# Two graph attention layers on one core: six row maxima of layer 1 moved into layer 0's fourth chunk, and one epilogue moved from GpSimd to VectorE

## The chip, the cores and the metric

The kernel runs on one core of one Trainium2 chip. The metric is the device time of one execution in microseconds (us); lower is better. Time before: 656.13 us, the median of 3 runs (655.10 to 657.52).

## What is computed

Two attention layers over one dense adjacency of 4096 x 4096 int32, each with a residual and a layer norm over 64 features.

```python
def _L0_gnn_ref(item_embs, entity_embs, adj, W, a):
    Wh = item_embs @ W
    We = entity_embs @ W
    scores = (Wh @ a1)[:, None] + (We @ a2)[None, :]
    e = jnp.where(scores > 0, scores, ALPHA * scores)
    e = jnp.where(adj > 0, e, NEG_BIG)
    attention = jax.nn.softmax(e, axis=1)
    return jax.nn.elu(attention @ entity_embs + item_embs)
...
def _L1_gnn_ref(x, edge_index, weight_w, weight_a, bias):
    wh = x @ weight_w
    e = (wh @ a_src)[:, None] + (wh @ a_dst)[None, :]
    e = jax.nn.leaky_relu(e, negative_slope=0.01)
    attention = jax.nn.softmax(jnp.where(edge_index > 0, e, NEG_INF), axis=1)
    return attention @ wh + bias
...
x = _layernorm(x + _L0_gnn_ref(x, L0_gnn_entity_embs, adj, L0_gnn_W, L0_gnn_a), axis=-1)
x = _layernorm(x + _L1_gnn_ref(x, adj, L1_gnn_weight_w, L1_gnn_weight_a, L1_gnn_bias), axis=-1)
```

## The kernel before

**Chunks and steps.** The 4096 rows of a layer are 32 tiles of 128 rows. A layer is done in five chunks of 4, 8, 8, 8 and 4 tiles (`WIDTHS`). Chunks are numbered through both layers: 0 to 4 are layer 0, 5 to 9 layer 1 (`NC` is 5). A chunk has 32 steps J, one for each tile of 128 columns of the adjacency. The position in the code of all that stands beside a step is written out by hand as "if J is so much".

**A step.** TensorE writes the mask of the step into PSUM (`zps`, line 1161): the adjacency in fp8 (`v`) times diagonals `D` of one value a row, 4 or 8 matmuls. Then the row score `S_row` and the column score go in, by one of two ways. In an unseeded step VectorE does it after the mask (`z`, line 990). In a seeded step ScalarE has written it before (a seed, line 718), and TensorE adds the mask to it. `SEEDS` has the number of seeded steps of each chunk. ScalarE takes the exponential into `Pm` (line 726), and TensorE multiplies it with the features (the product, lines 1106 and 1113) two steps later, in narrow chunks up to four or five. `zps` is a ring of three places of two banks; a narrow step takes one bank.

**Row maxima.** The diagonals of a chunk need for each row the maximum of `u` (the column scores) over its neighbours. `row_max(C, r, q)` (line 847, VectorE) takes it for row tile r of chunk C over one segment q of the 4096 columns, with `v` and `u_row` as inputs; `segments` has their bounds. Layer 0's `u_row` is known from the start. In layer 1 a piece of `u` is known only when its rows of layer 0 are finished, so chunks 5 and 6 have four and three segments. `pieces_at(C, J)` says which pieces stand at which step. The maxima of the next chunk are done during a chunk; before the change, those of layer 1 stand in chunk 4 and later, since both layers use the same `u_row`: the first loads of layer 1's `u` wait until layer 0's last maximum is done. `diagonals(C + 1)` follows at J=30, and TensorE begins the next chunk with them.

**The adjacency.** SP loads halves of row tiles (1 MB) into three buffers `adj_in`; VectorE (a compare, line 824) or ScalarE turns each into fp8 in `v`. In chunk 3 VectorE compares the eight halves of chunk 4's rows (`halves_at`, spread over 27 steps).

**The epilogue of a chunk** runs during the next one. ScalarE copies the sums out (`o`, J=4); GpSimd then adds the flags' part, multiplies with the reciprocal, and with relu and exponential by ScalarE makes the elu, subtracts the mean, squares, takes the power -0.5 of the variance (line 543) and scales (line 510). VectorE gives it the reciprocal (`reciprocal`), the sums (`sums`) and the squares (`squares`) at the steps in the tables `AFTER_WIDE`, `IN_LAST` (chunk 4) and `IN_FIRST` (chunk 5). With `scores` VectorE makes the next layer's scores of these rows (`uS`). At step `rows` TensorE turns `uS` (`turn_rows`, line 1025). Chunks 3 and 4 (`SPREAD`) have no time for a round through memory: VectorE makes diagonals of `u` (`u_diagonals`, line 904), TensorE spreads them (`spread_u`, line 1040), and ScalarE saves them in `u_row` (line 607). For chunks 0 to 2 the row goes to memory (`store_rows`) and is loaded to all partitions (`load_u`, line 420).

**What waits for what.** Each engine works through its own list in order. TensorE's `turn_rows` waits for `uS`, and every later mask and product stands behind it.

## Time and profile before

| | us |
|---|---|
| median of the runs | 656.13 |
| profiled execution | 654.75 |
| its span | 652.9 |
| VectorE, ScalarE, TensorE, GpSimd busy | 565.0, 522.3, 507.9, 180.6 |

The profile is of one execution. Busy shares are means over stages that differ, so a step is read in its own stretch. Times of rows are from the span's start. Chunk 3 begins (first exponential) at 258.5 us, chunk 4 at 325.1, chunk 5 at 382.8, chunk 6 at 435.9.

### The profile page before, as it was taken

How to read it: one execution, taken by the hardware profiler on the slowest of the kernel's cores; microseconds unless marked ns; L12 is line 12 of the kernel's file. 1: busy time of each engine (PE TensorE's matmuls, PEld its weight loads, DVE VectorE, ACT ScalarE, POOL GpSimd, SP SyncE). 2: the span in 40 equal slices, each digit the busy share in tenths (PEclk: the TensorE clock that was granted, in tenths of full speed). 3: DMA queues.
4: the chain of work that ended last, by engine and by line, in shares of the span. 5: the costliest groups of instructions: out<-in, count | busy, mean ns of one | idle time of the engine just before them, and what ended most of it. 6: DMA issues, size and time to landing. Idle time of an engine off the chain costs nothing. (4 is left out here: it accounts for less than half of the span.)

```text
span 652.9 us, 14284 instructions
## 1 busy us (share of the span) xinstructions
PE 507.9 (78%) x6039; PEld 236.0 (36%) x6039; DVE 565.0 (87%) x761; ACT 522.3 (80%) x606; POOL 180.6 (28%) x126
## 2 busy tenths in 40 slices
...
DMA packets 18252, 76.16 MB, mean 117 GB/s; under 512 B 6300, under 2 KB 8524, under 8 KB 9996
## 3 DMA queue, kind: packets, MB, share of 16 engines
...
q10 hardware_dynamic: 532, 0.08, 0.1%
q14 instruction: 17, 0.14, 0.1%
...
## 5 line engine op out<-in xcount | busy, mean ns | idle before, releaser
L726 ACT ACTIVATE Pm<-zps,ebias 128x1024 f32<-128x1024 f32 (+1 forms) x320 | 291.8, 934 | 75.0 <-DVE zps L990 47.4
L847 DVE CUSTOM_DVE_ANT_0 junk<-v,u_row 128x2048 int8<-128x2048 int8 (+4 forms) x144 | 308.1, 2159 | 3.3 <-ACT v L586 3.0
L1161 PE MATMUL zps<-D,v 128*128 128x128 bf16 x2048 | 166.5, 225 | 57.9 <-DVE D L867 27.7
L1161 PEld LDWEIGHTS zps<-D,v 128*128 128x128 fp8e4 x2048 | 119.5, 100 | 199.6 <-ACT zps L718 76.0
L718 ACT ACTIVATE zps<-S_row,ntau_col 128x1024 f32<-128x1024 f32 (+1 forms) x191 | 180.9, 949 | 5.1
L990 DVE SCALAR_TENSOR_TENSOR zps<-S_row,tau_col,zps 128x1024 f32<-128x1024 f32 (+1 forms) x129 | 135.0, 1064 | 42.8 <-PE zps L1161 42.0
L1106 PE MATMUL acc<-Pm,VE 128*32 128x512 f32 (+2 forms) x1280 | 150.5, 544 | 15.7 <-ACT Pm L726 13.1
L1106 PE MATMUL acc<-Pm,X 128*32 128x512 f32 (+2 forms) x1280 | 139.4, 524 | 20.8 <-ACT Pm L726 19.2
L1113 PE MATMUL acc<-Pm,ones 128*32 128x256 f32 (+1 forms) x1280 | 88.6, 350 | 0.0
L477 POOL TENSOR_TENSOR tAB<-flag,totW 128x520 f32<-128x520 f32 (+1 forms) x9 | 12.1, 1349 | 253.4 <-issue 161.6
L1113 PEld LDWEIGHTS acc<-Pm,ones 128*32 128x32 f32 x1280 | 43.5, 116 | 73.9 <-issue 64.9
L824 DVE TENSOR_SCALAR v<-adj_in 128x2048 fp8e4<-128x2048 int32 x44 | 61.7, 1405 | 1.9 <-DMA adj_in<-in_adj 1.8
L586 ACT ACTIVATE v<-adj_in,tanh_bias 128x2048 fp8e4<-128x2048 int32 x20 | 39.7, 2004 | 12.1 <-DMA adj_in<-in_adj 12.1
L1106 PEld LDWEIGHTS acc<-Pm,X 128*32 128x32 f32 x1280 | 28.3, 109 | 45.9 <-ACT Pm L726 31.7
L1106 PEld LDWEIGHTS acc<-Pm,VE 128*32 128x32 f32 x1280 | 27.5, 112 | 35.8 <-ACT Pm L726 22.2
L543 POOL TENSOR_TENSOR rstd<-var,mhalf 128x8 f32<-128x8 f32 (+1 forms) x10 | 21.9, 2192 | 45.1 <-DVE var L915 45.1
L506 POOL TENSOR_TENSOR tAB<-tAB,mean 128x512 f32<-128x512 f32 (+1 forms) x9 | 18.6, 2066 | 32.2 <-DVE mean L910 32.2
L489 POOL TENSOR_TENSOR o<-o,rden 128x512 f32<-128x512 f32 (+1 forms) x9 | 13.3, 1479 | 21.4 <-DVE rden L518 21.4
L485 POOL TENSOR_TENSOR o<-o,tAB 128x520 f32<-128x520 f32 (+1 forms) x9 | 12.4, 1378 | 21.3 <-ACT o L672 12.0
L507 POOL TENSOR_TENSOR tAB<-tAB 128x512 f32<-128x512 f32 (+1 forms) x9 | 16.2, 1804 | 0.7
L586 ACT ACT_TABLE_LOAD x1 | 1.3, 1283 | 18.4 <-DMA adj_in<-in_adj 18.4
L1025 PE MATMUL zps<-identf,uS 128*8 128x128 f32 (+1 forms) x5 | 1.6, 314 | 17.9 <-DVE uS L933 17.9
...
## 6 DMA issues: line engine op xcount, KB each, us to landing
...
S_row<-S_rows_scratch SPq DMA_DIRECT2D x3, 256.0 KB, 3.0
out<-tAB SPq DMA_DIRECT2D x3, 256.0 KB, 3.3
...
u_row<-u_row_scratch SPq DMA_DIRECT2D x2, 256.0 KB, 3.5
S_row<-S_rows_scratch POOLq DMA_DIRECT2D x1, 256.0 KB, 8.4
...
```

What stands on the lines that cost most here:

```text
L506: link(ns.tensor_tensor(tBf, tBf, per_row(mean[:, 0:n]), ALU.add))
L507: ns.tensor_tensor(tAf, tBf, tBf, ALU.mult).then_inc(sq_done, 1)
L543: g.tensor_tensor(rstd[:, 0:R(C)], var[:, 0:R(C)], mhalf[:, 0:R(C)], ALU.pow).then_inc(rstd_done, 1)
L586: a.activation(v[:, H // 2, H % 2 * HALF:(H % 2 + 1) * HALF], adj_in[:, H % AB, :], ACT.Tanh, bias=tanh_bias[:, :], scale=40.0, saturate=F ...
L718: a.activation(mask_of(n), S_row[:, C % 2, 0:R(C) * P], ACT.Relu, bias=ntau_col[:, layer(C), n % JT:n % JT + 1]).then_inc(seed_done, 1)
L726: a.activation(Pm_of(k, 0, R(C) * P), mask_of(k), ACT.Exp, bias=ebias[:, layer(C), int(seeded(k)), J:J + 1])\
L824: d.tensor_scalar(v[:, H // 2, H % 2 * HALF:(H % 2 + 1) * HALF], adj_in[:, H % AB, :], 0.0, 0.5, ALU.is_gt, ALU.subtract, saturate=False). ...
L847: d.tensor_tensor_reduce(out=junk[:, at % 2, 0:cols.stop - cols.start], in0=v_bytes[:, rt, cols], in1=u_row[:, cols], scale=1.0, scalar=-3 ...
L990: d.scalar_tensor_tensor(z, S_row[:, C % 2, 0:R(C) * P], tau_col[:, layer(C), J:J + 1], z, ALU.max, ALU.add).then_inc(z_done, 1)
L1106: last = t.matmul(acc[s * F + f:s * F + f + G, int(second), 0:cols], V[:, f:f + G], Pm_of(k, s * w, cols), start=first, stop=end)
L1113: last = t.matmul(acc[q * G:(q + 1) * G, 1, 0:w], ones[:, :], Pm_of(k, q * w, w), start=first, stop=end)
L1161: last = t.matmul(mask[:, r * P:(r + 1) * P], v[:, chunks[C][1] + r, J * P:(J + 1) * P], D[:, C % 2, PART * second + r, :], start=(r * P % ...
```

## The change

Layer 1's `u_row` gets a place of its own: the buffer of `adj_in` that half 61 was in, free once that half is converted. So six of the maxima of chunks 5 and 6, over the columns of chunks 0 and 1 (1536), stand in chunk 3 at `BEFORE_LAST`. Segments are cut at row 1536 instead of 1280 and 2048. Chunk 4's halves and maxima are spread over 20 steps of chunk 3 instead of 27 and 29. The epilogue of chunk 3 is done by VectorE: `epilogue` is split in `add_up`, `normalise` and `scale`, which stand at J=6, 10 and 15 of chunk 4; GpSimd keeps the power. `rows` goes from 23 to 20 in chunk 4 and from 17 to 20 in chunk 5. Chunk 3 has 20 seeded steps (16 before), chunk 5 has 20 (26 before). Unseeded are then in chunk 3 the steps 0 to 3, 5, 7, 11, 15, 19, 23, 27 and 28, in chunk 4 the steps 0, 1, 7, 8 and 22 to 25, in chunk 5 the steps 0 to 3, 6 to 8, 17 and 22 to 25.

```diff
-SEEDS = ((29, 28, 28, 16, 24), (26, 18, 18, 10, 0))
+SEEDS = ((29, 28, 28, 20, 24), (20, 18, 18, 10, 0))
...
-    IN_LAST = dict(reciprocal=6, elu=9, sums=13, squares=17, scores=21, rows=23)
-
-    IN_FIRST = dict(reciprocal=6, elu=8, sums=10, squares=13, scores=15, rows=17, maxima=19, second=21)
+    IN_LAST = dict(add_up=6, elu=8, normalise=10, scores=15, rows=20)
+
+    IN_FIRST = dict(reciprocal=6, elu=8, sums=10, squares=14, scores=18, rows=20, maxima=21, second=23)
...
-    EARLY = (4, 5, 7, 8, 9, 10, 11, 12, 14, 15, 18, 19, 22, 24)
+    BEFORE_LAST = (19, 20, 21, 23, 25, 27)
+    EARLY = (3, 4, 5, 7, 8, 11, 12, 13, 17, 19)
+    LATE_AT = 23
...
+    BY_VECTOR = (NC - 2, LAST)
...
-        u_row = sb("u_row", [P, N], BF16)
+        U1_AT = (2 * JT - 3) % AB
+        u_row = sb("u_row", [P, N], BF16), adj_in[:, U1_AT, :].bitcast(BF16)
...
-        um = sb("um", [P, 2, RT, Q])
+        um = sb("um", [P, 3, RT, Q])
...
+            third, first_spread = rows(2).start, rows(SPREAD[0]).start
             if C == NC:
-                first_spread = rows(SPREAD[0]).start
-                ends = [0, first_spread // 2, first_spread, KNOWN * P, N]
+                ends = [0, third, first_spread, KNOWN * P, N]
             elif C == NC + 1:
-                ends = [0, QW, KNOWN * P, N]
+                ends = [0, third, KNOWN * P, N]
...
-            return [h for h in range(first, end) if (h - first) * 27 // (end - first) == J]
+            return [h for h in range(first, end) if (h - first) * halves_within(C) // (end - first) == J]
+
+        def halves_within(C):
+
+            return 20 if C == NC - 2 else 27
+
+        known_first = [(NC, r, 0) for r in range(R(NC))] + [(NC + 1, r, 0) for r in range(R(NC + 1))]
...
+            if C == NC - 2:
+                n = 2 * R(nxt)
+                return [(nxt, i // 2, i % 2) for i in range(n) if i * halves_within(C) // n + 1 == J] + \
+                       [piece for piece, step in zip(known_first, BEFORE_LAST) if step == J]
             if C == NC - 1:
-                early = [(NC, r, q) for q in range(2) for r in range(R(NC))] + [(NC + 1, r, 0) for r in range(R(NC + 1))]
-                late = [(NC, r, 2) for r in range(R(NC))]
+                early = [(NC, r, 1) for r in range(R(NC))] + known_first[len(BEFORE_LAST):]
                 return [piece for piece, step in zip(early, EARLY) if step == J] + \
-                       [piece for i, piece in enumerate(late) if at("rows", C) + 2 + i == J]
+                       [(NC, r, 2) for r in range(R(NC)) if LATE_AT + r == J]
             if C == NC:
                 n = R(nxt)
-                open_ = [(nxt, r, 0) for r in range(len(EARLY) - 2 * R(NC), n)] + [(nxt, r, 1) for r in range(n)]
-                return [piece for i, piece in enumerate(open_) if 1 + i * 18 // len(open_) == J] + \
+                return [(nxt, r, 1) for r in range(n) if 1 + r * 18 // n == J] + \
                        [(NC, r, 3) for r in range(R(NC)) if at("maxima", C) + r // 2 == J] + \
...
             def load_u(C):
-                sp.dma_start(u_row[:, rows(C)], u_scr[rows(C)].rearrange("(one n) -> one n", one=1)
+                wait_v(sp, 2 * JT - 3)
+                sp.wait_ge(scr_written, written(max(C + 1, 2)))
+                sp.dma_start(u_row[1][:, rows(C)], u_scr[rows(C)].rearrange("(one n) -> one n", one=1)
                              .broadcast_to([P, R(C) * P])).then_inc(u_landed[C], 16)
...
+                if C == NC - 2:
+                    for c in range(2):
+                        load_u(c)
                 if 1 <= C < NC - 1:
                     store_rows(C - 1)
                     load_S(C + 1)
                 elif C == NC - 1:
-                    sp.wait_ge(max_done, 2 * JT)
-                    sp.wait_ge(scr_written, written(SPREAD[0]))
-                    for c in range(SPREAD[0]):
-                        load_u(c)
+                    load_u(2)
                     load_S(C + 1)
                     store_rows(C - 1)
...
+        def add_up(eng, ns, link, C):
...
-            if C == LAST:
+            if C in BY_VECTOR:
                 reciprocal(C)
...
+            ns.tensor_tensor(tBf, h, xs, ALU.add).then_inc((elu_in, y_done)[layer(C)], 1)
+
+        def normalise(eng, ns, link, C, sums, squares):
...
-            (squares if C == LAST else inverse)(C)
+            if C in BY_VECTOR:
+                squares(C)
+
+        def scale(eng, ns, C):
...
+            ns.tensor_tensor((xs, tBf)[layer(C)], tBf, per_row(rstd, C), ALU.mult).then_inc(new_done, 1)
...
-                if C == LAST:
+                if C in BY_VECTOR:
                     inverse(C)
-                else:
-                    epilogue(pool, g, link, C, inverse=inverse)
+                    continue
+                add_up(pool, g, link, C)
+                normalise(pool, g, link, C, None, None)
+                inverse(C)
+                scale(pool, g, C)
...
-                act.wait_ge(max_done, 2 * JT)
-                a.activation(u_row[:, rows(C)], zps[:, buf("u", C), 0:R(C) * P], ACT.Copy).then_inc(u_saved, 1)
+                wait_v(act, 2 * JT - 3)
+                a.activation(u_row[1][:, rows(C)], zps[:, buf("u", C), 0:R(C) * P], ACT.Copy).then_inc(u_saved, 1)
...
-                                       in0=v_bytes[:, rt, cols], in1=u_row[:, cols], scale=1.0, scalar=-3.0e38,
-                                       op0=ALU.mult, op1=ALU.max, accum_out=um[:, C % 2, r, q:q + 1])\
+                                       in0=v_bytes[:, rt, cols], in1=u_row[layer(C)][:, cols], scale=1.0, scalar=-3.0e38,
+                                       op0=ALU.mult, op1=ALU.max, accum_out=um[:, C % 3, r, q:q + 1])\
...
                 if C in SPREAD:
-                    xs = X[:, xc, 0:F]
-                    per_feature = [wbc[:, k, :].unsqueeze(1).broadcast_to([P, R(C), F]) for k in (2, 3)]
+                    if C in BY_VECTOR:
+                        scale(dve, d, C)
...
-                        if J == at("reciprocal", C) + BEHIND_FIRST * (C - 1 in FIRSTS):
+                        if J == at("add_up", C):
+                            add_up(dve, d, link, C - 1)
+                        if J == at("normalise", C):
+                            normalise(dve, d, link, C - 1, sums, squares)
+                        if at("reciprocal", C) and J == at("reciprocal", C) + BEHIND_FIRST * (C - 1 in FIRSTS):
```

VectorE, chunk 3, from the `z` of step 18 (before) or 19 (now) to the scores of chunk 2. `ISA junk,um` is a row maximum, `ISA um` its read-out, `v<-adj_in` a compare. Before:

```order
L990 SCALAR_TENSOR_TENSOR zps<-S_row,tau_col,zps 128x1024
L847 ISA junk,um<-v,u_row 128x2048
L847 ISA um 128x1
L824 TENSOR_SCALAR v<-adj_in 128x2048
L990 SCALAR_TENSOR_TENSOR zps<-S_row,tau_col,zps 128x1024
L928 TENSOR_REDUCE s_col<-tAB 128x8
L930 TENSOR_REDUCE t_col<-tAB 128x8
L932 TENSOR_SCALAR uS<-t_col,uoff 128x8
L933 TENSOR_SCALAR uS<-s_col 128x8
L847 ISA junk,um<-v,u_row 128x2048
L847 ISA um 128x1
L990 SCALAR_TENSOR_TENSOR zps<-S_row,tau_col,zps 128x1024
```

Now:

```order
L1027 SCALAR_TENSOR_TENSOR zps<-S_row,tau_col,zps 128x1024
L879 ISA junk,um<-v,adj_in 128x1536
L879 ISA um 128x1
L879 ISA junk,um<-v,adj_in 128x1536
L879 ISA um 128x1
L879 ISA junk,um<-v,adj_in 128x1536
L879 ISA um 128x1
L961 TENSOR_REDUCE s_col<-tAB 128x8
L963 TENSOR_REDUCE t_col<-tAB 128x8
L965 TENSOR_SCALAR uS<-t_col,uoff 128x8
L966 TENSOR_SCALAR uS<-s_col 128x8
L1027 SCALAR_TENSOR_TENSOR zps<-S_row,tau_col,zps 128x1024
```

Three maxima over 1536 columns, whose row lies in `adj_in`, stand ahead of the scores; the compare and the maximum over 2048 columns that stood there went to earlier steps.

VectorE, chunk 4, from J=6. `rden` is the reciprocal, `tAB` and `o` are the epilogue's tiles. Before:

```order
L518 RECIPROCAL rden<-o 128x8
L990 SCALAR_TENSOR_TENSOR zps<-S_row,tau_col,zps 128x512
L847 ISA junk,um<-v,u_row 128x1280
L847 ISA um 128x1
L990 SCALAR_TENSOR_TENSOR zps<-S_row,tau_col,zps 128x512
L847 ISA junk,um<-v,u_row 128x1280
L847 ISA um 128x1
L847 ISA junk,um<-v,u_row 128x1280
L847 ISA um 128x1
L847 ISA junk,um<-v,u_row 128x1280
L847 ISA um 128x1
L847 ISA junk,um<-v,u_row 128x1280
```

Now:

```order
L498 TENSOR_TENSOR tAB<-flag,totW 128x520
L506 TENSOR_TENSOR o<-o,tAB 128x520
L542 RECIPROCAL rden<-o 128x8
L510 TENSOR_TENSOR o<-o,rden 128x8x64
L515 TENSOR_TENSOR tAB<-o,X 128x512
L1027 SCALAR_TENSOR_TENSOR zps<-S_row,tau_col,zps 128x512
L879 ISA junk,um<-v,adj_in 128x1024
L879 ISA um 128x1
L1027 SCALAR_TENSOR_TENSOR zps<-S_row,tau_col,zps 128x512
L879 ISA junk,um<-v,adj_in 128x1536
L879 ISA um 128x1
L522 TENSOR_TENSOR tAB<-tAB 128x512
```

Four passes of the epilogue stand around the reciprocal, and the first of `normalise` after two more maxima.

VectorE, chunk 4, ahead of the row scores that TensorE turns (`s_col`, `t_col`, `uS`). Before:

```order
L914 TENSOR_REDUCE tot<-tAB 128x8
L915 TENSOR_SCALAR var<-tot 128x8
L847 ISA junk,um<-v,u_row 128x2048
L847 ISA um 128x1
L847 ISA junk,um<-v,u_row 128x2048
L847 ISA um 128x1
L925 TENSOR_TENSOR tAB<-X,wbc 128x8x64
L926 TENSOR_TENSOR tAB<-X,wbc 128x512
L928 TENSOR_REDUCE s_col<-tAB 128x8
L930 TENSOR_REDUCE t_col<-tAB 128x8
L932 TENSOR_SCALAR uS<-t_col,uoff 128x8
L933 TENSOR_SCALAR uS<-s_col 128x8
```

Now:

```order
L879 ISA junk,um<-v,adj_in 128x1536
L879 ISA um 128x1
L879 ISA junk,um<-v,adj_in 128x1536
L879 ISA um 128x1
L538 TENSOR_TENSOR X<-tAB,rstd 128x8x64
L958 TENSOR_TENSOR tAB<-X,wbc 128x8x64
L959 TENSOR_TENSOR tAB<-X,wbc 128x512
L961 TENSOR_REDUCE s_col<-tAB 128x8
L963 TENSOR_REDUCE t_col<-tAB 128x8
L965 TENSOR_SCALAR uS<-t_col,uoff 128x8
L966 TENSOR_SCALAR uS<-s_col 128x8
L936 TENSOR_TENSOR D<-identb,uS 128x1024
```

`X<-tAB,rstd` (the scaling) came from GpSimd's list, and the squares stand three maxima ahead instead of two. On TensorE the turning of `uS` and the spreading of `u` stand before the masks of steps 20 and 21, not between those of steps 22 and 23.

## Rows read from the trace of the kernel before

**Rows 1.** The page, part 1: busy time, share of the span and instructions of each engine.
```profile
PE 507.9 (78%) x6039; PEld 236.0 (36%) x6039; DVE 565.0 (87%) x761; ACT 522.3 (80%) x606; POOL 180.6 (28%) x126
```

**Rows 2.** Busy time by stretch: length, each engine's busy us, TensorE's granted clock, DMA, GB/s.
```profile
258.50:325.07 66.57, 64.54 (x774) 28.62 (x775) 53.82 (x60) 54.90 (x58) 20.12 (x13) 1.00 0.30 98
325.07:382.80 57.73, 38.29 (x635) 23.05 (x631) 48.25 (x73) 38.73 (x64) 23.95 (x12) 0.87 0.04 11
382.80:435.90 53.10, 34.88 (x447) 17.05 (x440) 43.09 (x102) 36.94 (x64) 14.60 (x11) 0.88 0.04 11
...
356.50:367.90 11.40, 1.87 (x11) 0.84 (x15) 10.19 (x18) 0.70 (x2) 5.29 (x2) 0.56 0.00 0
```

**Rows 3.** The timeline of TensorE, chunks 3, 4 and 5: start, duration, line, idle before.
```profile
309.98 1.07 PE L1106 MATMUL acc<-Pm,VE 128*32 128x512 f32 x8
...
365.07 0.38 PE L1025 MATMUL zps<-identf,uS 128*8 128x128 f32 x1 [10.97 <-DVE uS L933]
...
412.49 0.37 PE L1025 MATMUL zps<-identf,uS 128*4 128x128 f32 x1 [6.89 <-DVE uS L933]
```

**Rows 4.** The timeline of ScalarE, chunk 4.
```profile
333.17 0.19 ACT L672 ACTIVATE o<-zps 128x8 f32<-128x8 f32 x1
...
340.41 0.63 ACT L680 ACTIVATE o<-tAB 128x512 f32<-128x512 f32 x1
340.95 0.67 ACT L718 ACTIVATE zps<-S_row,ntau_col 128x512 f32<-128x512 f32 x1
341.56 0.67 ACT L726 ACTIVATE Pm<-zps,ebias 128x512 f32<-128x512 f32 x1
...
368.65 1.00 ACT L607 ACTIVATE u_row<-zps 128x1024 bf16<-128x1024 f32 x1
```

**Rows 5.** The timeline of GpSimd, chunks 3 and 4.
```profile
301.27 1.19 POOL L514 TENSOR_TENSOR tAB<-X,wbc 128x512 f32<-128x512 f32 x1
...
356.67 3.76 POOL L543 TENSOR_TENSOR rstd<-var,mhalf 128x8 f32<-128x8 f32 x1 [1.00 <-DVE var L915]
360.51 1.53 POOL L510 TENSOR_TENSOR X<-tAB,rstd 128x512 f32<-128x512 f32 x1
```

**Rows 6.** The timeline of VectorE, chunk 4: scores of chunk 3 and what follows.
```profile
362.07 0.69 DVE L925 TENSOR_TENSOR tAB<-X,wbc 128x512 f32<-128x512 f32 x1 [0.93 <-POOL X L510]
...
364.71 0.23 DVE L932 TENSOR_SCALAR uS<-t_col,uoff 128x8 f32<-128x8 f32 x1
...
367.06 2.28 DVE L847 CUSTOM_DVE_ANT_0 junk<-v,u_row 128x2048 int8<-128x2048 int8 x1
...
380.58 0.73 DVE L867 TENSOR_SCALAR D<-identb,g 128x128 bf16<-128x128 bf16 x4
```

**Rows 7.** The same timeline: one instruction of each kind that is counted.
```profile
291.44 1.28 DVE L990 SCALAR_TENSOR_TENSOR zps<-S_row,tau_col,zps 128x1024 f32<-128x1024 f32 x1
...
372.25 1.22 DVE L847 CUSTOM_DVE_ANT_0 junk<-v,u_row 128x1024 int8<-128x1024 int8 x1
...
373.40 0.75 DVE L990 SCALAR_TENSOR_TENSOR zps<-S_row,tau_col,zps 128x512 f32<-128x512 f32 x1
...
389.40 2.28 DVE L847 CUSTOM_DVE_ANT_0 junk<-v,u_row 128x2048 int8<-128x2048 int8 x1
...
394.80 1.76 DVE L847 CUSTOM_DVE_ANT_0 junk<-v,u_row 128x1536 int8<-128x1536 int8 x1
```

**Rows 8.** VectorE's waits from 258.5 to 301 (us, times, longest); a slowed maximum; the scores.
```profile
DVE zps L990 <- PE zps L1161: 4.2, 5, 1.4
...
282.13 3.20 DVE L847 CUSTOM_DVE_ANT_0 junk<-v,u_row 128x2048 int8<-128x2048 int8 x1
...
301.93 0.68 DVE L928 TENSOR_REDUCE s_col<-tAB 128x8 f32<-128x512 f32 x1
```

**Rows 9.** The page, part 6: issues, KB each, median us to landing.
```profile
u_row<-u_row_scratch SPq DMA_DIRECT2D x2, 256.0 KB, 3.5
```

**Rows 10.** The timeline of VectorE, end of chunk 5.
```profile
432.30 1.39 DVE L867 TENSOR_SCALAR D<-identb,g 128x128 bf16<-128x128 bf16 x8
```

More of the change, by code:

```diff
@@ L457, in _, with tiles_of, per_row, per_feature @@
             sp.wait_ge(out_written, stored(LAST))
-        def epilogue(eng, ns, link, C, sums=None, squares=None, inverse=None):
+        def tiles_of(C):
             n = R(C)
-            b3 = [P, n, F]
-            xs = X[:, xcols(C), 0:F]
-            h, tAf, tBf = o[:, 0:n, 0:F], tA[:, 0:n, 0:F], tB[:, 0:n, :]
-            def per_row(t):
-                return t.unsqueeze(2).broadcast_to(b3)
-            def per_feature(t):
-                return t.unsqueeze(1).broadcast_to(b3)
+            return X[:, xcols(C), 0:F], o[:, 0:n, 0:F], tA[:, 0:n, 0:F], tB[:, 0:n, :]
+        def per_row(t, C):
+            return t[:, 0:R(C)].unsqueeze(2).broadcast_to([P, R(C), F])
+        def per_feature(t, C):
+            return t.unsqueeze(1).broadcast_to([P, R(C), F])
+        def add_up(eng, ns, link, C):
+            n = R(C)
+            xs, h, tAf, tBf = tiles_of(C)
             eng.wait_ge(totW_saved, layer(C) + 1)
@@ L500, in epilogue @@
                 ns.tensor_tensor(tBf, tBf, h, ALU.add).then_inc(y_done, 1)
-            else:
-                ns.tensor_tensor(tBf, h, xs, ALU.add).then_inc(y_done, 1)
-            if C == LAST:
+            if C in BY_VECTOR:
                 sums(C)
             eng.wait_ge(mean_done, C + 1)
-            link(ns.tensor_tensor(tBf, tBf, per_row(mean[:, 0:n]), ALU.add))
+            link(ns.tensor_tensor(tBf, tBf, per_row(mean, C), ALU.add))
             ns.tensor_tensor(tAf, tBf, tBf, ALU.mult).then_inc(sq_done, 1)
-            (squares if C == LAST else inverse)(C)
+            if C in BY_VECTOR:
+                squares(C)
+        def scale(eng, ns, C):
+            xs, h, tAf, tBf = tiles_of(C)
             eng.wait_ge(rstd_done, C + 1)
-            ns.tensor_tensor(xs if layer(C) == 0 else tBf, tBf, per_row(rstd[:, 0:n]), ALU.mult).then_inc(new_done, 1)
-            if layer(C) == 0 and C not in SPREAD:
-                eng.wait_ge(new_done, C + 1)
-                ns.tensor_tensor(tAf, xs, per_feature(wbc[:, 2, :]), ALU.mult).then_inc(sprod_done, 1)
-                ns.tensor_tensor(tBf, xs, per_feature(wbc[:, 3, :]), ALU.mult).then_inc(tprod_done, 1)
+            ns.tensor_tensor((xs, tBf)[layer(C)], tBf, per_row(rstd, C), ALU.mult).then_inc(new_done, 1)
         def reciprocal(C):
@@ L565, in _ @@
                     g.memset(columns_of_ones, 1.0).then_inc(ones_set, 1)
-                if C == LAST:
+                if C in BY_VECTOR:
                     inverse(C)
-                else:
-                    epilogue(pool, g, link, C, inverse=inverse)
+                    continue
[3 more added lines that the diff above has]
+                scale(pool, g, C)
+                if layer(C) == 0 and C not in SPREAD:
+                    xs, h, tAf, tBf = tiles_of(C)
+                    pool.wait_ge(new_done, C + 1)
+                    g.tensor_tensor(tAf, xs, per_feature(wbc[:, 2, :], C), ALU.mult).then_inc(sprod_done, 1)
+                    g.tensor_tensor(tBf, xs, per_feature(wbc[:, 3, :], C), ALU.mult).then_inc(tprod_done, 1)
         @block.scalar
```

19 lines of the change are left out of this document (12 added, 7 removed).

## The prediction

> **What bounds the kernel now.** I read the page's busy shares first [rows 1]: VectorE is busy for 87% of the span, ScalarE 80%, TensorE 78%, and no one of them is the bound everywhere. So I cut the span where ScalarE's first exponential of a chunk begins and asked for busy times by stretch [rows 2]. Chunk 3 (258.5 to 325.1 us) belongs to TensorE: 64.5 of 66.6 us busy at full clock, with VectorE at 53.8 and ScalarE at 54.9. Chunk 4 (325.1 to 382.8) belongs to nobody: TensorE 38.3 of 57.7, VectorE 48.3, ScalarE 38.7. In its stretch from 356.5 to 367.9, TensorE works 1.9 us and ScalarE 0.7. Chunk 5 (53.1 us) is alike.
>
> TensorE's waits name what is missing [rows 3]: it stands before line 1025, the turning of the row scores, for `uS` of VectorE, 10.97 us in chunk 4 (at J=23, from 354.10 to 365.07) and 6.89 us in chunk 5 (at J=17, until 412.49). `uS` is the end of chunk 3's epilogue: sums by ScalarE at 333.36 (333.17 + 0.19) [rows 4], then GpSimd until 362.04 (360.51 + 1.53) [rows 5], then the scores on VectorE, 362.07 to 364.94 [rows 6]. So GpSimd and its partners take 28.7 us for ten operations: its last pass of 128x512 took 1.53 us and the power of eight elements a row 3.76, while VectorE runs a pass of 128x512 in 0.69 [rows 5, 6].
>
> **The change in chunk 4, the term that decides.** I step along VectorE, the engine that now carries both jobs, with durations from [rows 6, 7], less some 0.08 by which one overlaps the next (372.25 + 1.22 is 373.47, the next starts at 373.40): a maximum over 1024 columns 1.14 us, over 1536 1.68, over 2048 2.20; `z` of 512 columns 0.66, of 1024 columns 1.19; a pass of 128x512 0.61, or 0.70 where it is linked, so that the next waits for its end (an estimate from the 0.69).
> - Until J=6 it does three maxima of 1024 in place of two of 1280, and is free by 330.1. The first product with the flags (0.7) fits before ScalarE's 333.36. Then add 0.7, reciprocal 0.25, multiply 0.7, add 0.6: 335.6.
> - J=7 to 9: two `z` and maxima of 1024 and 1536: 4.15 us, 339.8. ScalarE's relu is not done before 340.4 [rows 4], and its exponential by 341.0.
> - `normalise` at J=10: three passes (2.0), sums (0.9), two passes (1.3), squares (0.9) from 340.4: 345.6.
> - GpSimd's power: 3.76 us in [rows 5], beside VectorE's work, so to 349.4. Three maxima of 1536 (5.1) cover it: 350.7. That cover is thin by 1.3 us; without it VectorE would wait.
> - `scale` 0.7, two products 1.2, scores and `uS` as in [rows 6] 1.6: ready at 354.2, not 364.9. TensorE, now stopped at J=20, gets there some 3 us earlier than to J=23 (a seeded step takes ScalarE 1.3 us, [rows 4]), so it stands 3 to 4 us, not 11.
> - From there VectorE has the diagonals of `u` and the columns (2.2, from 364.9 to 367.1 in [rows 6]), two maxima of 1536 (3.4), four `z` (2.6), four maxima of 1024 (4.6), and `diagonals(5)` with its terms (2.4): 369.4. I add 0.7 for small gaps. The copy of `u` that the last four wait for ended at 369.65, 4.7 us after `uS` [rows 4, 6], so by 358.9, before VectorE asks for it at 361. Diagonals ready at 370.1 against 381.2 [rows 6]: **-11.1 us**. ScalarE has 12 exponentials (0.67) and six seeds (0.63) left after 357.2, 12 us, and ends at 369 to 370: no later. What is late next is VectorE itself.
>
> In columns, chunk 4 loses 8x1280 + 6x2048 and gains 4x1024 + 6x1536; the 9216 columns that are saved (about 10 us) went to chunk 3.
>
> **Chunk 3.** VectorE gets six maxima of 1536 (+10.1) and four fewer `z` of 1024 columns (-4.8); ScalarE four more seeds (+4.2, on 54.9 of 66.6). In sum it fits under TensorE. Where it may not: chunk 4's halves and maxima are pressed into 20 steps. Up to `scores` at J=22 VectorE has two more maxima of 2048 (4.4), one more compare (1.1), three new maxima (5.1), and three fewer `z` (-3.6): +7.0 us. The waits for TensorE before it, 4.2 us in five [rows 8], swallow some: it comes to `scores` 2.8 us later than at 301.9 [rows 8], near 305. Then `z` of step 23 is done near 308, its exponential near 309, and TensorE needs it at 310 (the product of step 23 at 309.98) [rows 3]. It fits barely; I take **+1.0 us**. Bounds: below, 0, since TensorE is already at 97%; above, the contention with GpSimd. A maximum of 2048 took 3.20 us at 282.13, beside GpSimd's passes, against 2.28 at 389.40 [rows 7, 8]. Six more slowed by 0.92 are 5.5, so +5.
> The Trainium skill (GPSIMD Engine Reference, 8. Key points) says that GpSimd contends with VectorE instructions that have two SBUF inputs or run in a two-port mode. The moved maxima have two such inputs, so by that rule all six pay if GpSimd works beside each, and the sum would be -4.6, not -10. The trace agrees that there is a price, but three of the six stand after GpSimd's last pass, which ended at 302.5 [rows 5].
>
> Loading: two of the three rows of `u` now leave SP at chunk 3's end of loads, before `store_rows(2)` and `load_S(4)`. They land in 3.5 us [rows 9], issued once half 61 is compared (J=12, about 283) and half 63 is issued, and are wanted at J=19, about 298. The third follows `store_rows(2)` and is wanted at chunk 4's J=3. Nothing waits, and `store_rows(2)` comes after both.
>
> **Chunk 5.** Six fewer seeds: ScalarE -3.8, VectorE +4.0 (six `z` of 0.66). VectorE was idle 10.0 of 53.1 us [rows 2]. The maxima keep their 16384 columns. Scores stand at J=18, behind two maxima of 2048 and the `z` of step 17: counted as above from the chunk's first exponential, `uS` is ready at +31.7 instead of +29.6 (412.4, [rows 3]). TensorE's wait grows from 6.9 to 8 or 9 us. But two maxima of 1536 that stood behind the scores (3.4 us) are done before. So the four maxima of 512 end at +38.8 (as before), and `diagonals(6)` at +51.0 (before +50.9, [rows 10]). **0 us**; bounds -2 (TensorE's low clock at its start goes) and +3 (VectorE full). Chunks 6 to 9 keep their order and durations: 0.
>
> **Sum:** -11.1 + 1.0 + 0 = -10.1, taken as -10. The profiled execution, 654.75 us around its span of 652.9, would take 644.8. The median of the runs is 656.13, 1.4 higher; by the same difference I predict 646.1. A measurement of this kernel can tell about 0.5%, 3.3 us, from no change: so faster means under 652.8.
>
> **The rivals.**
> - *Forecast*, -7 to -14: 0.72.
> - *VectorE in chunk 4 is late itself.* The ten passes cost 1.0 instead of 0.7, or GpSimd's power is not covered: `uS` at 359. The gain is half, -5, with chunk 3's +1: -4, 652.1. For it: 48.3 of 57.7 us were busy before. Against it: 28.7 us of epilogue shrink to some 7 us of passes, three reductions and one power. 0.11.
> - *Given back in chunks 3 and 5.* Chunk 3 +5, chunk 5 +4 (each `z` that leaves ScalarE lands in VectorE's chain): -2, 654.1. For it: `uS` in chunk 5 is late already. 0.10.
> - *Slower, through chunk 3.* Before J=22 stand 11 maxima and 8 compares. If all met GpSimd and lost 0.92 (for a compare an estimate from the maximum's): 19x0.92 = 17.5 us, of which three times 0.92 are there now. Less 1.5 us slack, TensorE would stand some 13 us in the one chunk that it bounds, and work after it at 1.2 GHz: the granted clock is 0.56 in the stretch of the 11 us wait, against 1.00 in chunk 3 [rows 2]. Ten us at the lower level cost 5. +18 - 11 = +7, 663. It decides from about 11 us lost in chunk 3. Against it: GpSimd is busy for 20.1 us of that chunk, and of its sixteen maxima and compares it slowed only three. 0.05. The Trainium skill (TensorE: Matmul & The Clock Gate, Part 1) has it that the low clock is the default and activity lifts it; the granted clocks above agree.
> - *The change doesn't do what it says*: the row of `u` lands late and VectorE stands at J=19. It must be 15 us late to matter. 0.02.
>
> **Numbers.** Faster: 0.72, and 0.08 of the second case. Same: the third, the rest of the second, half of the last: 0.14. Slower: 0.06. The range takes 641.5 (-14.6: chunk 5 gives 2, the clock stays up in chunk 4) to 653.0 (-3.1, second case and its surroundings); it leaves out the third and fourth, and tails.
>
> **What would show it.** TensorE's wait for `uS` in chunk 4 of 3 to 4 us, not 11; chunk 4 near 47 us long; chunk 3 66.6 to 69; chunk 5 53; in chunk 5 a longer wait; VectorE's maxima in chunk 4 all uncontended; GpSimd with ten ops fewer. Wrong if chunk 3 lengthens by over 5, if `uS` in chunk 4 comes later than 357, or if chunk 5 lengthens.

## The result, and the profile after

The changed kernel takes 652.12 us, median of 13 runs (649.99 to 653.74), against 656.02 for the kernel before, 13 runs beside it (652.40 to 657.52): a ratio of 0.9942, 95% interval 0.9926 to 0.9958. It is faster, by 3.9 us or 0.6%. The forecast was a gain of 10 us, 646.1. The profiled execution took 650.33 us, its span 648.5 against 652.9.

Busy times by stretch of the changed kernel, cut at the first exponential of chunks 3, 4, 5, 6 and 7. The columns are those of [rows 2]: length, TensorE's matmuls and weight loads, VectorE, ScalarE, GpSimd, granted clock, DMA.

```profile
258.20:329.89 71.69, 66.35 (x778) 29.21 (x775) 61.63 (x68) 59.44 (x63) 24.55 (x13) 0.98 0.28 91
329.89:375.60 45.71, 36.63 (x636) 23.10 (x637) 40.42 (x75) 38.45 (x65) 3.26 (x2) 0.96 0.04 13
375.60:428.69 53.09, 34.24 (x423) 17.03 (x420) 45.22 (x100) 35.72 (x62) 13.86 (x11) 0.84 0.03 11
428.69:494.14 65.45, 58.27 (x548) 23.25 (x544) 56.91 (x66) 55.19 (x57) 14.04 (x10) 0.92 0.04 11
```

Chunk 6 of the kernel before, the same view:

```profile
435.90:498.60 62.70, 53.09 (x536) 21.27 (x538) 56.95 (x66) 55.27 (x56) 14.03 (x10) 1.00 0.03 12
```

| | before | after | forecast | measured |
|---|---|---|---|---|
| chunk 3 | 66.6 | 71.7 | +1.0 (0 to +5) | +5.1 |
| chunk 4 | 57.7 | 45.7 | -11.1 | -12.0 |
| chunk 5 | 53.1 | 53.1 | 0 | 0.0 |
| chunk 6 | 62.7 | 65.4 | 0 | +2.8 |

With -0.3 us before chunk 3 that is -4.4, the difference of the spans. Chunks 7 to 9 are as they were. So the gain is where it was forecast, and a little larger; more than half of it is given back in two places, ahead of it and behind it.

**Chunk 4, the gain.** TensorE's two waits for `uS` in the changed kernel's timeline, which answer to [rows 3]:

```profile
358.57 0.27 PE L1064 MATMUL zps<-identf,uS 128*8 128x128 f32 x1 [3.64 <-DVE uS L966]
...
406.47 0.37 PE L1064 MATMUL zps<-identf,uS 128*4 128x128 f32 x1 [6.59 <-DVE uS L966]
```

3.64 us instead of 10.97, where 3 to 4 were expected.

**Chunk 3, the first loss.** VectorE around the scores of chunk 2, the changed kernel's timeline. L879 is a row maximum, L1027 a `z`, L961 the first reduction of `scores`:

```profile
275.94 3.25 DVE L879 CUSTOM_DVE_ANT_0 junk<-v,u_row 128x2048 int8<-128x2048 int8 x1
...
281.83 2.96 DVE L879 CUSTOM_DVE_ANT_0 junk<-v,u_row 128x2048 int8<-128x2048 int8 x1
...
300.78 2.66 DVE L879 CUSTOM_DVE_ANT_0 junk<-v,adj_in 128x1536 int8<-128x1536 int8 x1
...
303.37 2.73 DVE L879 CUSTOM_DVE_ANT_0 junk<-v,adj_in 128x1536 int8<-128x1536 int8 x1
...
306.03 1.75 DVE L879 CUSTOM_DVE_ANT_0 junk<-v,adj_in 128x1536 int8<-128x1536 int8 x1
...
307.71 0.67 DVE L961 TENSOR_REDUCE s_col<-tAB 128x8 f32<-128x512 f32 x1
...
309.35 1.28 DVE L1027 SCALAR_TENSOR_TENSOR zps<-S_row,tau_col,zps 128x1024 f32<-128x1024 f32 x1
```

ScalarE and TensorE behind it (L758 is the exponential, L750 a seed, L1145 the product, L1200 the mask):

```profile
310.67 1.12 ACT L758 ACTIVATE Pm<-zps,ebias 128x1024 f32<-128x1024 f32 x1 [3.27 <-DVE zps L1027]
311.81 1.12 ACT L750 ACTIVATE zps<-S_row,ntau_col 128x1024 f32<-128x1024 f32 x1
```

```profile
302.07 1.06 PE L1145 MATMUL acc<-Pm,VE 128*32 128x512 f32 x8 [1.38 <-ACT Pm L758]
...
312.99 1.03 PE L1200 MATMUL zps<-D,v 128*128 128x128 bf16 x8 [2.96 <-ACT zps L750]
```

The same mask in the kernel before:

```profile
309.43 0.62 PE L1161 MATMUL zps<-D,v 128*128 128x128 bf16 x8 [1.06 <-ACT zps L718]
```

VectorE reaches the scores at 307.7, not 305. The `z` of step 23 stands behind them; ScalarE waits 3.27 us for it, and its next seed, that of step 25, stands in ScalarE's list behind the exponential of step 23. TensorE waits for that seed: 2.96 us in the chunk that it bounds. The two waits make 4.3 us, and for 3.4 us from 312.5 the granted clock was low (0.98 on average over the chunk), worth up to 1.7. The wait of 1.1 us that stood at this place before is in the new one. 4.3 + 1.7 - 1.1 is 4.9 of the 5.1 us, an estimate, since the low clock may have cost less.

**Chunk 6, the second loss.** The table has chunk 5 at 53.1 us in both kernels, but inside it the changed one is ahead: its last exponential starts 48.1 us after its first (before 51.3). What sets the chunk's length is VectorE: the diagonals of chunk 6 are ready 50.4 us after the first exponential (before 50.9), and TensorE's first mask of chunk 6 waits for them. ScalarE waits behind it, in the changed kernel:

```profile
428.69 1.11 ACT L758 ACTIVATE Pm<-zps,ebias 128x1024 f32<-128x1024 f32 x1 [4.32 <-DVE zps L1027]
```

```profile
426.08 1.03 PE L1200 MATMUL zps<-D,v 128*128 128x128 bf16 x8 [2.06 <-DVE D L899]
```

Four stretches of the changed kernel: just before TensorE's clock falls, until it rises, the beginning of chunk 6, and a second fall inside it:

```profile
414.90:418.40 3.50, 1.59 (x28) 0.82 (x24) 3.33 (x15) 1.25 (x3) 0.00 (x0) 0.99 0.00 0
418.40:432.00 13.60, 10.67 (x91) 4.54 (x84) 9.79 (x32) 6.69 (x12) 0.00 (x0) 0.50 0.11 40
428.69:445.60 16.91, 14.57 (x112) 6.78 (x104) 12.87 (x11) 10.50 (x15) 0.00 (x0) 0.70 0.00 1
438.80:445.60 6.80, 6.80 (x41) 2.94 (x38) 4.93 (x5) 5.04 (x8) 0.00 (x0) 0.50 0.01 2
```

And the places in the kernel before that answer to the first three:

```profile
422.60:426.00 3.40, 1.76 (x28) 0.90 (x25) 3.12 (x16) 1.17 (x3) 0.00 (x0) 1.00 0.00 0
426.00:439.70 13.70, 10.68 (x138) 5.22 (x139) 12.00 (x34) 11.42 (x18) 0.00 (x0) 1.00 0.12 39
435.90:452.80 16.90, 13.20 (x140) 6.17 (x138) 15.58 (x14) 13.15 (x17) 2.50 (x3) 1.00 0.00 1
```

### The profile page after: what moved, and what is told of

Read it like the earlier page. It is cut to its first block, busy times and chain, and to the rows that moved or that the text cites. A ratio compares the mean times of both kernels' runs of the same rounds, so it can differ in the third digit from the quotient of the medians.

```text
span 648.5 us, 14276 instructions
## 1 busy us (share of the span) xinstructions
PE 511.5 (79%) x6037; PEld 237.8 (37%) x6039; DVE 567.1 (87%) x769; ACT 525.5 (81%) x608; POOL 163.6 (25%) x116
## 4 chain that ended last, share of the span: by engine, by line
DVE 28%; issue 26%; PE 19%; ACT 14%; POOL 6%; DMA 5%; SPq 1%; POOLq 0%; ACTq 0%; DVEq 0%
DVE junk L879 13%; PE acc L1145 10%; ACT Pm L758 10%; DVE zps L1027 7%; PE zps L1200 6%; DMA adj_in<-in_adj 5%; PE acc L1152 2%; DVE v L856 2%; ACT v L618 2%; ACT zps L750 1%; POOL o L506 1%; DVE tot L941 1%; POOL rstd L567 1%; POOL tAB L522 1%; DVE tot L946 1%
## 5 line engine op out<-in xcount | busy, mean ns | idle before, releaser
L758 ACT ACTIVATE Pm<-zps,ebias 128x1024 f32<-128x1024 f32 (+1 forms) x320 | 291.7, 936 | 68.5 <-DVE zps L1027 55.3
L1200 PE MATMUL zps<-D,v 128*128 128x128 bf16 x2048 | 168.2, 226 | 58.9 <-DVE D L899 27.9
L1200 PEld LDWEIGHTS zps<-D,v 128*128 128x128 fp8e4 x2048 | 121.0, 100 | 200.6 <-ACT zps L750 81.0
L750 ACT ACTIVATE zps<-S_row,ntau_col 128x1024 f32<-128x1024 f32 (+1 forms) x193 | 183.9, 955 | 5.1
L1027 DVE SCALAR_TENSOR_TENSOR zps<-S_row,tau_col,zps 128x1024 f32<-128x1024 f32 (+1 forms) x127 | 131.2, 1053 | 42.3 <-PE zps L1200 41.7
L1145 PE MATMUL acc<-Pm,VE 128*32 128x512 f32 (+2 forms) x1280 | 149.3, 540 | 16.3 <-ACT Pm L758 12.8
L1145 PE MATMUL acc<-Pm,X 128*32 128x512 f32 (+2 forms) x1280 | 143.4, 538 | 19.5 <-ACT Pm L758 18.0
L879 DVE CUSTOM_DVE_ANT_0 junk<-v,adj_in 128x2048 int8<-128x2048 int8 (+3 forms) x80 | 153.7, 1947 | 2.1 <-ACT adj_in L639 1.7
L879 DVE CUSTOM_DVE_ANT_0 junk<-v,u_row 128x2048 int8<-128x2048 int8 x64 | 152.6, 2398 | 2.5 <-ACT v L618 2.3
L1152 PEld LDWEIGHTS acc<-Pm,ones 128*32 128x32 f32 x1280 | 43.2, 115 | 73.2 <-issue 63.6
L1145 PEld LDWEIGHTS acc<-Pm,X 128*32 128x32 f32 x1280 | 28.9, 111 | 45.7 <-ACT Pm L758 30.4
L1145 PEld LDWEIGHTS acc<-Pm,VE 128*32 128x32 f32 x1280 | 27.3, 110 | 36.7 <-ACT Pm L758 24.1
L510 POOL TENSOR_TENSOR o<-o,rden 128x512 f32<-128x512 f32 (+1 forms) x8 | 10.8, 1346 | 24.4 <-DVE rden L542 24.4
L515 POOL TENSOR_TENSOR tAB<-o,X 128x512 f32<-128x512 f32 (+1 forms) x8 | 13.4, 1676 | 0.6
```

Of the source, the lines that this page charges most:

```text
L750: a.activation(mask_of(n), S_row[:, C % 2, 0:R(C) * P], ACT.Relu, bias=ntau_col[:, layer(C), n % JT:n % JT + 1]).then_inc(seed_done, 1)
L758: a.activation(Pm_of(k, 0, R(C) * P), mask_of(k), ACT.Exp, bias=ebias[:, layer(C), int(seeded(k)), J:J + 1])\
L879: d.tensor_tensor_reduce(out=junk[:, at % 2, 0:cols.stop - cols.start], in0=v_bytes[:, rt, cols], in1=u_row[layer(C)][:, cols], scale=1.0, ...
L1027: d.scalar_tensor_tensor(z, S_row[:, C % 2, 0:R(C) * P], tau_col[:, layer(C), J:J + 1], z, ALU.max, ALU.add).then_inc(z_done, 1)
L1145: last = t.matmul(acc[s * F + f:s * F + f + G, int(second), 0:cols], V[:, f:f + G], Pm_of(k, s * w, cols), start=first, stop=end)
L1152: last = t.matmul(acc[q * G:(q + 1) * G, 1, 0:w], ones[:, :], Pm_of(k, q * w, w), start=first, stop=end)
```

## The experiments

Theory 1 for chunk 3: the place of three maxima, ahead of the scores and beside GpSimd, costs the 5 us. Its rival: VectorE is full, wherever they stand. For chunk 4: which of the two edits, the maxima or the epilogue, made the gain. For chunk 6: the clock, or something that it accompanies. All ratios are to the kernel before, run beside.

### The maxima behind the scores

```diff
-    BEFORE_LAST = (19, 20, 21, 23, 25, 27)
+    BEFORE_LAST = (23, 24, 25, 26, 27, 28)
```

> The changed kernel, with the six moved maxima at J=23 to 28 of chunk 3, behind the scores of chunk 2, not at 19 to 27 with three of them ahead. Theory 1 (what costs chunk 3 its 5.1 us is that three maxima, two of them slowed by GpSimd from 1.68 to 2.6 and 2.7 us, stand ahead of the z of step 23, on which ScalarE's next seed and TensorE wait): VectorE reaches the scores some 5 us earlier, chunk 3 takes 66.6 to 68 us and not 71.7, none of the six maxima takes over 1.8 us, and the kernel is 3 to 5 us faster than the changed one (about 648). Theory 2 (VectorE is simply full in chunk 3 with six more maxima, wherever they stand): chunk 3 stays at 70 to 72 us and the time at 652.

647.08 us, ratio 0.9889 (0.9867 to 0.9912): some 0.5% better than the changed kernel, and the intervals do not overlap. (The profiled execution came to chunk 3 2.3 us later than that of the changed kernel, with the same code ahead of it. So lengths of chunks are compared, not spans.) Chunks 3 and 4:

```profile
260.50:328.10 67.60, 65.09 (x778) 28.74 (x775) 60.07 (x68) 59.36 (x63) 23.03 (x13) 1.00 0.30 97
328.10:374.10 46.00, 36.85 (x634) 23.16 (x635) 40.41 (x75) 38.39 (x64) 3.26 (x2) 0.93 0.04 13
```

All six moved maxima took 1.75 us. Chunk 3 is 1.0 us over the kernel before, with 6.3 us more of VectorE's work in it. Theory 1 holds; VectorE had the room. The halves and maxima of chunk 4 are still pressed into 20 steps here, so that is not what cost the 5 us.

### Chunk 2's two products on VectorE

The two GpSimd passes that ran beside the slowed maxima are taken away, and the maxima left where the change has them.

```diff
-                if layer(C) == 0 and C not in SPREAD:
+                if layer(C) == 0 and C < NC - 3:
...
-                if C in SPREAD:
+                if C in (NC - 3, NC - 2, NC - 1):
```

> The changed kernel (three moved maxima ahead of the scores), but the two products with the score weights in chunk 2's epilogue are VectorE's, as for chunks 3 and 4, not GpSimd's. These two passes ran beside the two slowed maxima. Theory 1 (GpSimd's passes slow the maxima): the maxima at J=19 and 20 take 1.75 us instead of 2.66 and 2.73; VectorE gains 1.9 and pays 1.2 for the products; chunk 3 is 70 to 71.5 us. Theory 2 (the maxima are slowed by something else, such as the adjacency's loads or the row's new place in adj_in): they stay at 2.6 to 2.7 us, and chunk 3 takes 72 to 73 us.

650.02 us, ratio 0.9919 (0.9892 to 0.9946). The maxima of J=19 and 20:

```profile
300.68 1.75 DVE L879 CUSTOM_DVE_ANT_0 junk<-v,adj_in 128x1536 int8<-128x1536 int8 x1
...
302.35 1.75 DVE L879 CUSTOM_DVE_ANT_0 junk<-v,adj_in 128x1536 int8<-128x1536 int8 x1
```

Theory 1 holds. The two were slowed by GpSimd, by 0.91 and 0.98 us, and by nothing else: the row in `adj_in` costs nothing. The Trainium skill (GPSIMD Engine Reference, 8. Key points) names this contention for instructions with two SBUF inputs; the trace agrees. Chunk 3 takes 70.8 us, 0.9 less, with 1.2 us of products added on VectorE. From that I estimate that the contention of these two is worth some 2 us. With the maxima behind the scores the chunk was 4.1 us shorter, so their place ahead of the scores is worth the other 2.

### Chunk 3 with its 16 seeds, maxima behind the scores

```diff
-SEEDS = ((29, 28, 28, 20, 24), (20, 18, 18, 10, 0))
+SEEDS = ((29, 28, 28, 16, 24), (20, 18, 18, 10, 0))
...
-    BEFORE_LAST = (19, 20, 21, 23, 25, 27)
+    BEFORE_LAST = (23, 24, 25, 26, 27, 28)
```

> As a_behind_scores, with 16 seeded steps in chunk 3 as before, not 20. VectorE gets four z of 1024 columns back (4.8 us), ScalarE loses four seeds. Theory 1 (behind the scores VectorE has room): chunk 3 67 to 69 us, the time within 1.5 us of a. Theory 2 (the four seeds are what made room for the six maxima): chunk 3 over 70 us and the time 3 to 5 us above a.

648.60 us, ratio 0.9909 (0.9888 to 0.9930). Chunk 3 takes 68.5 us, 0.9 more than with 20 seeds. In the profile the four seeds are worth about 1 us; the ratios, 0.9909 and 0.9889, overlap. The seeds are not what made room.

### The epilogue back on GpSimd, the maxima moved

```diff
-    IN_LAST = dict(add_up=6, elu=8, normalise=10, scores=15, rows=20)
+    IN_LAST = dict(reciprocal=6, elu=9, sums=13, squares=17, scores=21, rows=23)
...
-    LATE_AT = 23
+    LATE_AT = 25
...
-    BY_VECTOR = (NC - 2, LAST)
+    BY_VECTOR = (LAST,)
```

> The changed kernel, with the epilogue of chunk 3 back on GpSimd, its steps as before (reciprocal 6, elu 9, sums 13, squares 17, scores 21, rows 23) and the third segment's maxima at J=25 to 28. The moved maxima stay moved. Theory 1 (chunk 4's 12 us come from the epilogue on VectorE, which shortens TensorE's wait): TensorE waits 8 to 11 us for uS again, chunk 4 takes 54 to 57 us, time 661 to 663, slower than both kernels, since chunk 3's 5 us are paid for nothing. Theory 2 (they come from the 9216 columns of maxima that left chunk 4): chunk 4 takes 47 to 50 us and the time is near 654.

659.64 us, ratio 1.0070 (1.0041 to 1.0099): slower than both.

### The epilogue on VectorE, no maximum moved to chunk 3

```diff
-SEEDS = ((29, 28, 28, 20, 24), (20, 18, 18, 10, 0))
+SEEDS = ((29, 28, 28, 16, 24), (20, 18, 18, 10, 0))
...
-    BEFORE_LAST = (19, 20, 21, 23, 25, 27)
-    EARLY = (3, 4, 5, 7, 8, 11, 12, 13, 17, 19)
+    BEFORE_LAST = ()
+    EARLY = (3, 4, 5, 7, 8, 9, 11, 12, 13, 14, 16, 17, 18, 19, 21, 22)
...
-            return 20 if C == NC - 2 else 27
+            return 27
...
-                return [(nxt, i // 2, i % 2) for i in range(n) if i * halves_within(C) // n + 1 == J] + \
+                return [(nxt, i // 2, i % 2) for i in range(n) if i * 29 // n + 1 == J] + \
```

> The changed kernel, with no maximum moved to chunk 3: all sixteen stand in chunk 4 (J=3 to 22), chunk 3 has its 16 seeds, 27 and 29 steps of before; the epilogue is on VectorE. Theory 1 (the epilogue alone gives chunk 4 its gain, while VectorE has the room): chunk 3 takes 66.6 us again; VectorE gets 10 us of maxima in chunk 4, of which some 5 stand ahead of uS, so chunk 4 takes 52 to 56 us and the time is 653 to 656. Theory 2 (the epilogue is the whole gain and the maxima's place does not matter): chunk 4 at 46 to 48 us, time 647 to 648.

655.62 us, ratio 1.0012 (0.9994 to 1.0029): no difference from the kernel before. Chunk 4 of the two last kernels, the one with GpSimd's epilogue and the one with all maxima in chunk 4, and TensorE's longest wait in each:

```profile
331.80:384.10 52.30, 37.92 (x630) 23.36 (x631) 35.71 (x65) 38.77 (x64) 19.50 (x12) 0.90 0.03 12
...
PE zps L1064 <- DVE uS L966: 5.5, 1, 5.5
```

```profile
326.70:382.80 56.10, 39.96 (x646) 24.09 (x643) 50.41 (x88) 38.65 (x65) 3.26 (x2) 0.88 0.03 11
...
PE zps L1064 <- DVE uS L966: 7.3, 1, 7.3
```

Against 57.7 us, the moved maxima alone give 5.4, the epilogue alone 1.6, both together 12.0: 5 us more than the sum. The epilogue on VectorE needs the time that the moved maxima free; while they stand in chunk 4, VectorE has 50.4 us of work in 56.1 and `uS` is late again. With only the maxima gone, VectorE is at 35.7 us, and it waits four times for GpSimd's epilogue, 10.0 us in all. For the kernel with GpSimd's epilogue neither theory had the size right: I expected TensorE to wait 8 to 11 us, and it waited 5.5. For the other one theory 1 holds, at its edge: 56.1 us (52 to 56 expected), and 655.62 (653 to 656).

### Chunk 5: its seeds, its steps

Three kernels. With 26 seeds in chunk 5 (and the changed kernel's chunk 3):

```diff
-SEEDS = ((29, 28, 28, 20, 24), (20, 18, 18, 10, 0))
+SEEDS = ((29, 28, 28, 20, 24), (26, 18, 18, 10, 0))
```

> The changed kernel, with 26 seeded steps in chunk 5 as before, not 20. Theory 1 (the later z on VectorE make scores and uS of chunk 4 late, and TensorE's low clock at the end of chunk 5 costs chunk 6 its 2.8 us): chunk 5 ends some 2 us earlier, the granted clock at the start of chunk 6 may be full, and the time falls by 1 to 4 us. Theory 2 (the seeds of chunk 5 are worth nothing either way, VectorE's maxima and diagonals at its end set it): chunks 5 and 6 together stay within 1 us of 118.5, time 652.

With the maxima behind the scores, 26 seeds and the steps of before:

```diff
-SEEDS = ((29, 28, 28, 20, 24), (20, 18, 18, 10, 0))
+SEEDS = ((29, 28, 28, 20, 24), (26, 18, 18, 10, 0))
...
-    IN_FIRST = dict(reciprocal=6, elu=8, sums=10, squares=14, scores=18, rows=20, maxima=21, second=23)
+    IN_FIRST = dict(reciprocal=6, elu=8, sums=10, squares=13, scores=15, rows=17, maxima=19, second=21)
...
-    BEFORE_LAST = (19, 20, 21, 23, 25, 27)
+    BEFORE_LAST = (23, 24, 25, 26, 27, 28)
```

> As a_behind_scores, but chunk 5 as before the change: 26 seeds, squares, scores, rows, maxima and second at J=13, 15, 17, 19 and 21. Against a_behind_scores (chunks 5 and 6: 53.1 and 65.4 us; before the change 53.1 and 62.7). Theory 1 (chunk 6 is 2.8 us longer because TensorE is left with so little work at the end of chunk 5 that its clock is at 1.2 GHz when chunk 6 begins, which follows from the new table of chunk 5): chunk 5 53 us, chunk 6 near 62.7 with the granted clock full at its start, 1 to 3 us faster than a. Theory 2 (the clock at chunk 6's start has nothing to do with chunk 5's table): chunk 6 stays at 65 us, and the time within 1 us of a.

The same steps with 20 seeds (the diff above without the line of `SEEDS`):

> As a_behind_scores, but chunk 5's steps of before (13, 15, 17, 19, 21), with its new 20 seeds. Tells the two halves of chunk 5's edit apart. If the steps are what lowers the clock: chunk 6 near 62.7 us as in e_a_first_as_before, and the time 1 to 3 us under a. If the seeds are: chunk 6 65 us.

| | chunk 5 | chunk 6 | sum | time | ratio (95%) |
|---|---|---|---|---|---|
| before | 53.1 | 62.7 | 115.8 | 656.02 | 1 |
| changed | 53.1 | 65.4 | 118.5 | 652.12 | 0.9942 (0.9926 to 0.9958) |
| maxima behind the scores | 53.1 | 65.4 | 118.5 | 647.08 | 0.9889 (0.9867 to 0.9912) |
| changed, 26 seeds | 51.4 | 65.9 | 117.3 | 651.11 | 0.9938 (0.9917 to 0.9960) |
| behind, steps of before | 52.4 | 64.4 | 116.8 | 645.47 | 0.9845 (0.9820 to 0.9870) |
| behind, steps and seeds of before | 51.3 | 63.7 | 115.0 | 644.50 | 0.9833 (0.9812 to 0.9853) |

The chunk 5 that the change brought is a loss of 0.56% in the ratios of the third and the last row, whose intervals do not overlap, and of 3.5 us in their profiles. Half of it in the profiles, and most of it in the ratios, comes back with the steps of before (though the interval of that row overlaps those of both its neighbours). The seeds alone make no difference that the runs can tell (fourth row against second, last against fifth), though the profiles have them at 1.2 and 1.8 us. Chunk 6 came back only in part, to 63.7 and 64.4 us where I had expected 62.7 if the steps were the cause.

The 3.5 us are not a fixed price. Two kernels from above, the one with the products on VectorE and the one with 16 seeds in chunk 3, have the changed kernel's chunk 5 as it is. In their profiles chunks 5 and 6 take 116.1 us together, not 118.5. This is chunk 6 with the products on VectorE:

```profile
427.75:491.53 63.78, 54.17 (x548) 21.64 (x544) 56.96 (x66) 55.32 (x56) 14.03 (x10) 0.99 0.04 12
```

The low clock ends 0.7 us into that chunk, not 3.3, and the second fall isn't there. Instead both have 3.4 us of low clock in chunk 8, which takes 56.8 us, not 55.3. So the low clock falls at different places from one profile to the next, and one profile doesn't give its mean price.

The last row is faster than both kernels: the change without its edit of chunk 5, and with the maxima behind the scores.

### TensorE kept busy at the end of chunk 5

```diff
+                    if C == NC and J > 21:
+                        for _ in range(8):
+                            t.matmul(acc[:, 1, 3 * P:4 * P], onesb[:, :], identb[:, :], start=True, stop=True,
+                                     skip_group_check=True)
                     if seeded(k):
```

on the kernel with the maxima behind the scores.

> As a_behind_scores, with eight matmuls of 128x128 ahead of each mask of steps 22 to 31 of chunk 5, into a part of the PSUM bank that nothing reads: the work that is computed stays the same, and TensorE is busier by some 0.45 us a step. Theory 1 (the low clock is the 2.8 us of chunk 6): the granted clock stays full from step 22 on, chunk 6 takes 62.7 us, and the time falls by 2 to 4 us against a. Theory 2 (the low clock is a companion of something else that is late, such as VectorE's diagonals or ScalarE's seeds): clock full, chunk 6 still 65 us, time unchanged; or the extra matmuls cost more than they give, +2 to +4 us.

646.63 us, ratio 0.9869 (0.9845 to 0.9893). In the profile, the stretch that answers to 418.4 to 432.0 above, and chunk 6:

```profile
415.40:429.10 13.70, 10.26 (x160) 5.97 (x152) 12.00 (x36) 8.56 (x14) 0.00 (x0) 1.00 0.11 39
...
426.80:489.50 62.70, 53.06 (x535) 21.24 (x536) 56.99 (x67) 55.31 (x57) 14.02 (x10) 1.00 0.04 12
```

Chunk 6 is at the 62.7 us of before, with nothing changed but extra work for TensorE, and the granted clock is full. In these profiles the clock is the whole of chunk 6's loss. In the timed runs little of it arrives: 0.9869 and 0.9889 are 0.2% apart and overlap, and the 2 to 4 us that theory 1 had expected didn't come. The profile has part of the reason. The filling costs 0.5 us in chunk 5, and chunk 8, whose code is the same, takes 1.4 us more than in the kernel without filling, at a lower clock. Here is chunk 8 with the filling:

```profile
551.68:608.43 56.75, 51.88 (x510) 20.25 (x511) 49.10 (x54) 46.42 (x46) 9.45 (x8) 0.97 0.02 6
```

and without it:

```profile
554.86:610.16 55.30, 50.41 (x510) 19.72 (x511) 49.00 (x54) 46.22 (x45) 9.46 (x8) 1.00 0.03 6
```

Over whole executions, the granted clock of the six runs averages 0.958 with the filling and 0.957 without (the kernel before, beside them: 0.958 and 0.960). The 20.4 us of low clock that went from the end of chunk 5 and from chunk 6 in the profile would make 0.016, an estimate. So the filling shows where chunk 6's time went in the profile; in the runs most of that low clock stands elsewhere or was not there.

The same filling on the fastest kernel:

> As e_a_first_as_before (maxima behind the scores, chunk 5 as before the change), with the eight extra matmuls ahead of each mask of steps 22 to 31 of chunk 5, as in g_a_filled. e has chunk 6 at 63.7 us with a low clock of 3.4 us just ahead of it and 6.8 us in it. If that clock is what is left of chunk 6's loss: chunk 6 62.7 us, the time 0.5 to 1.5 us under e. If the extra matmuls stand in the way of chunk 5, which has less slack here: chunk 5 0.5 to 2 us longer and no gain.

643.75 us, ratio 0.9840 (0.9819 to 0.9861), against 0.9833 without it: no difference. The low clock ahead of chunk 6 went, that of 6.8 us inside it stayed, and chunk 6 took 63.6 us. The filling doesn't reach it, and no run shows what causes it.

## Why the prediction was wrong

It said 646.1 us, a gain of 10; the gain was 3.9. The sign was right and the range, 641.5 to 653.0, holds the result near its end; two terms of the sum were wrong. That the range holds is luck. The rival "VectorE in chunk 4 is late itself" gave 652.1, nearly the time measured, by a mechanism that did not happen: `uS` was on time.

- **Chunk 4, -11.1: right.** Measured -12.0. `uS` was ready 28.6 us after the chunk's first exponential, by the forecast's steps 29.1. TensorE's wait was 3.64 us. Every step along VectorE held, the cover of GpSimd's power too (3.15 us, under three maxima).
- **Chunk 3, "It fits barely; I take +1.0 us": the step that failed.** Measured +5.1, past the upper bound, and past the "over 5" that was to show the forecast wrong. The contention with GpSimd stood only in the bound; the term itself had none. VectorE came to the scores at 307.7 and not at 305, since four maxima and two compares ahead of them were slowed beside GpSimd's passes, by 5.3 us in all, where the kernel before lost 2.5. And of the 4.2 us of waits that were to swallow its extra work, 0.8 stayed. The argument against it was "three of the six stand after GpSimd's last pass"; the other three are those ahead of the scores, and two of them paid 0.91 and 0.98 us. And I asked only when TensorE needs the product of step 23. It needs the mask of step 25 first, which waits for a seed that stands in ScalarE's list behind the exponential of step 23. The kernel before already waited 1.06 us there. So there was no slack of 1.5 us, and 2.96 us of waiting, with 3.4 us of low clock behind it. With the maxima behind the scores chunk 3 comes to the +1.0 that I had taken.
- **Chunk 5, 0: right as a length.** Measured 0.0, with the diagonals of chunk 6 ready at +50.4 (forecast +51.0), `uS` at +30.8 (forecast +31.7) and TensorE's wait 6.6 us, not 8 to 9.
- **"Chunks 6 to 9 keep their order and durations: 0": the second step that failed**, for chunk 6, +2.8 us. Order and work are the same; the clock is not. I had looked for the low clock in chunk 5's wait alone, and as a gift. It was no rival's mechanism. The rival "given back in chunks 3 and 5" had chunk 3's +5 as measured; its +4 of chunk 5 did not come.
- **The rival of chunk 3 with TensorE's clock** was of the right kind and the wrong size: 3 us of standing, not 13, and 3.4 us of low clock, not 10.
- **The term of the maxima was sized without the epilogue.** The forecast named the 9216 columns beside the term and not in it. Taken alone each part gives 5.4 and 1.6 us, together 12.0.
